# Exponent of an attention pass issued behind the FFN work that is woven into the same pass

## The reference, cut to what matters

```python
qkv    = einsum('nlck,cki->nlci', layernorm(x), Wqkv) + bqkv
scores = einsum('nlcd,nled->nldce', q, k) / 8      # 32x32 for each of 64 d
attn   = softmax(scores, axis=-1)
ctx    = einsum('nldcm,nlcd->nldm', attn, v)
x      = x + layernorm(ctx @ Wout + bout)          # per channel
gate, up = xn @ w_gate.T, xn @ w_up.T              # hidden 8192, xn = layernorm(x)
x      = x + layernorm((silu(gate) * up) @ w_down.T)
```

## Time and profile before

| | us |
|---|---|
| median of 3 runs | 7090.63 (7042.11 to 7113.12) |
| profiled execution, device time | 6908.24 |
| its span, slowest core (4) | 6906.7 (all cores 6886.3 to 6906.7) |
| mean granted TensorE clock of the cores | 0.797 to 0.801 |

### The profile page before, as it was taken

The page is one execution under the profiler, slowest core; times in us unless marked ns, Lnnn a source line. Parts: engine busy times, 40 slices in busy tenths (PEclk is TensorE's granted clock), DMA queues, the critical chain, the costliest instruction groups (busy, mean ns, idle before and its releaser), DMA issues.

```text
span 6906.7 us, 47532 instructions; the slowest of 8 cores (6886.3 to 6906.7 us)
## 1 busy us (share of the span) xinstructions
PE 3316.8 (48%) x15536; PEld 1510.1 (22%) x15536; DVE 3227.3 (47%) x3680; ACT 2051.3 (30%) x2953; POOL 16.4 (0%) x34
## 2 busy tenths in 40 slices
PE   0000011011076767650776767506858576069994
PEld 0000000000032323220333333203323232034441
DVE  0000026866756554637555546475655565631112
ACT  0000024344333434332333343324343433222110
POOL 0000000000000000000000000000000000000000
PEclk9999999555587888875787878757879787579997
DMA  9999940000042323221322322212313222134442
GB/s 112 110 109 109 109 56 6 1 6 6 0 122 73 101 83 104 79 64 34 107 89 79 104 87 96 62 36 92 104 61 122 70 101 68 36 113 143 153 141 88
DMA packets 177940, 558.92 MB, mean 81 GB/s; under 512 B 49568, under 2 KB 65952, under 8 KB 174496
## 3 DMA queue, kind: packets, MB, share of 16 engines
q1 hardware_dynamic: 171840, 444.69, 19.7%
q0 software_dynamic: 5856, 111.18, 14.4%
HBM read 641.83 MB, written 125.83 MB: 111 GB/s over the span
## 4 chain that ended last, share of the span: by engine, by line
DVE 31%; PE 23%; ACT 17%; another core or an unknown queue 14%; issue 9%; DMA 6%; DVEq 1%; ACTq 0%; SPq 0%
PE dps L415 10%; DVE es_sb L321 7%; DVE ctx_sb L330 6%; PE gps L353 5%; ACT es_sb L765 5%; PE ups L363 5%; DVE zs_sb L743 4%; DVE zs_sb L737 4%; DVE es_sb L728 3%; DMA wd_sb<-wdc 3%; ACT kd_sb L262 2%; ACT m_sb L379 2%; ACT e_sb L376 2%; DMA x2s_sb<-x2h 2%
## 5 line engine op out<-in xcount | busy, mean ns | idle before, releaser
L353 PE MATMUL gps<-xn_sb,wg_sb 128*128 128x512 bf16 x4096 | 1106.6, 432 | 347.8 <-DVE gated_sb L388 332.8
L415 PE MATMUL dps<-gated_sb,wd_sb 128*128 128x512 bf16 x4096 | 928.8, 385 | 100.7 <-DMA wd_sb<-wdc 49.2
L765 ACT ACTIVATE es_sb<-es_sb 128x4096 bf16<-128x4096 bf16 x256 | 921.9, 3601 | 23.1 <-DVE es_sb L728 23.1
L363 PE MATMUL ups<-xn_sb,wu_sb 128*128 128x512 bf16 x4096 | 925.8, 379 | 0.0
L249 PE MATMUL mps<-xn_sb,wqkv_sb 128*128 128x128 bf16 x512 | 72.3, 302 | 1511.2 <-DVE xn_sb L795 1460.0
L754 ACT ACTIVATE rz_sb<-zf_sb 128x128 bf16<-128x128 bf16 x256 | 79.0, 308 | 2343.3 <-DVE zf_sb L747 2343.3
L383 DVE TENSOR_TENSOR t_sb<-m_sb,gps 128x512 bf16<-128x512 bf16 x256 | 176.1, 688 | 1232.5 <-ACT m_sb L379 1232.5
L202 DVE TENSOR_SCALAR st_sb<-mps 1x128 f32<-1x128 f32 x48 | 13.4, 278 | 1441.4 <-PE mps L189 1441.4
L353 PEld LDWEIGHTS gps<-xn_sb,wg_sb 128*128 128x128 bf16 x4096 | 437.2, 108 | 987.7 <-issue 629.0
L321 DVE TENSOR_TENSOR es_sb<-es_sb,u_sb 128x4096 bf16<-128x4096 bf16 x256 | 586.8, 2292 | 28.4 <-DVE u_sb L312 2.3
L728 DVE TENSOR_TENSOR es_sb<-q_sb,kd_sb 128x4096 bf16<-128x4096 bf16 x256 | 586.0, 2290 | 24.4 <-DVE ctx_sb L330 0.9
(11 more groups left out here) (84 smaller groups left out, 2028.0 us busy)
## 6 DMA issues: line engine op xcount, KB each, us to landing
wg_sb<-wgc SPq DMA_DIRECT2D x256, 512.0 KB, 3.5
wu_sb<-wuc SPq DMA_DIRECT2D x256, 512.0 KB, 3.4
wd_sb<-wdc SPq DMA_DIRECT2D x256, 512.0 KB, 3.4
wgc<-wgH POOLq DMA_DIRECT2D x4, 8192.0 KB, 438.8
wuc<-wuH POOLq DMA_DIRECT2D x4, 8192.0 KB, 514.8
wdc<-wdH POOLq DMA_DIRECT2D x4, 8192.0 KB, 591.0
yT<-outs_sb SPq DMA_DIRECT2D x64, 256.0 KB, 2.9
xb_sb<-xH POOLq DMA_DIRECT2D x16, 512.0 KB, 8.6
```

The lines of the kernel that those rows point to most:

```text
L353: return tn.matmul(out=gps[pb].ap(), lhsT=wg_sb[pb].ap()[:, ft * 128:(ft + 1) * 128], rhs=xn2_sb.ap()[:, ft * W:(ft + 1) * W], start=(ft = ...
L363: return tn.matmul(out=ups[pb].ap(), lhsT=wu_sb[pb].ap()[:, ft * 128:(ft + 1) * 128], rhs=xn2_sb.ap()[:, ft * W:(ft + 1) * W], start=(ft = ...
L415: return tn.matmul(out=dps[pb].ap(), lhsT=wd_sb[wb].ap()[:, sh * 128:(sh + 1) * 128], rhs=gated_sb.ap()[:, ht * W:(ht + 1) * W], start=(ht ...
L765: ta = plan.op("A", lambda a, buf=buf: a.activation(out=buf.ap(), in_=buf.ap(), func=AF.Exp, scale=0.125), deps=[last[f"s_{c}_{j}"]], inc="A")
```

## The change

`emit_exp(j)` moves from ahead of `pull(2)` to behind `pull(2)` and `emit_uP(c, j - 1)`:

```diff
                 if j >= 1:
                     emit_z(j - 1)
                     emit_rz(j - 1)
-                if j < NJ:
-                    emit_exp(j)
                 pull(2)
                 if j >= 1:
                     emit_uP(c, j - 1)
+                if j < NJ:
+                    emit_exp(j)
```

## The result

| | us |
|---|---|
| changed kernel, median of 9 runs | 6597.89 (6585.88 to 6766.36) |
| kernel before, median of 10 runs | 6916.89 (6903.4 to 7113.12) |
| ratio of the two | 0.9551, 95% interval 0.9527 to 0.9574 |
| changed kernel, profiled execution, its span | 6596.17, 6594.6 |

By the ratio the change takes 4.5% off. The medians differ by 319 us, the profiled executions by 312; 315 had been forecast. In some executions of either kernel the cores of one die, sometimes of both, show a lower granted clock and the time is 1 to 3% longer; the three runs known of before, 7042 to 7113 us, were as long as such executions, and the ratio leaves these out.

The account below looks back on a forecast made before the run. In gu passes a loop of waits through ACT and DVE was the bound, not PE. 3 windows x (101.4 + 3.5) = 315 us, taken from the runs' median 7090.6, gave 6776 us, range 6670 to 6880.

Parts of the forecast that it names:

- The 182 us: Whole kernel: the runs' median lies 182 us above the profiled execution; carried over unchanged, may shrink or grow by some 100.
- the gain of a pass: Passes with two gu atoms: their first ACT instruction starts 3.50 us earlier, so a pass takes 17.08 us instead of 20.58.
- the cover: Gu passes: DVE's t1, gated, uP(j-1) and s(j+1) hide the moved exponent before z(j), with 5.3 us left over.
- the count: Gu passes of a window: 28 gain 3.5 us and 2 gain 1.7 us, 101.4 us a window.
- pass 0: First pass of a chunk with gu atoms: no gain, and no loss, with 0.7 us to spare before z(0).
- the second chunk from pass 1 to 9: Pass 1 moves the start of the down matmuls 3.5 us; first-half down passes, set by PE, and pass 9 gain zero.
- PE between two ends: Gu passes: PE idles 3.1 us at the high clock level, some 0.3 us at the low; the chain stays the bound.
- A: Rival: PE becomes the bound of the gu passes, 18.5 us a pass; gain 190 us, 6900 us; chance 0.06.
- B: Rival: granted clock falls to 0.80 in all dense stretches; 6940 us profiled, 7123 on the runs' scale; chance 0.05.
- C: Rival: z(j) waits for the moved exponent and the 3.5 us come back; 7091 us; chance 0.03.
- D: Rival: PE's clock stays at the low level in gu passes; +640 us, 7730 us; chance 0.02.
- ln4, bc4, down: Other passes: ln4 zero, the bc4 pass gains 3.5 us, first-half down passes cost zero, or 14 us in all if uncovered.

Follow-up runs that it names:

- e7: Kernel before, its order kept, with 6 further ACT instructions ahead of the exponent in gu passes from j = 1: 7288.1 us profiled, against 6912.7.
- e6: Changed order with 12 further ACT instructions ahead of the late exponent in gu passes from j = 1: 6905.0 us, ratio 0.9993 to the kernel before.
- e4: Against the kernel before, both atoms issued right after z(j-1), ahead of rz(j-1) and the exponent: 6317.2 us, ratio 0.9154.
- e2: Against the kernel before, the exponent issued late only in passes whose atoms contain a gu: 6605.0 us, ratio 0.9554.
- e3: Against the kernel before, the exponent issued late only in passes without a gu atom: 6924.8 us, ratio 0.9994.

## Why the prediction was right or wrong

**Wrong: the time itself.** 6776 us was forecast, 6670 to 6880 as its range; measured is 6598. The step that failed is the last of the sum: "I carry the difference over as it is". The 182 us between the profiled execution and the median of three runs were no property of the kernel. Of ten runs of before six lie at 6903 to 6919, by the profiled execution at 6908, and the other four, the three known runs among them, at 7042 and more. Had the sum ended on the profiled execution, 6593, it would have missed by 5 us. The hint was there: the profiled execution lay 134 us under the lowest of the runs, whose own spread is 71. The range let the 182 us shrink by some 100; they went altogether. With a difference like that unexplained, the range had to reach down to 6593; it stopped 77 us above. The mechanism and the gain were right.

**Right: the gain of a pass.** 3.50 us from the row of the exponent's place; passes went from 20.58 to 17.08 us. e7 shows the same from the other side.

**Right: the cover.** 5.3 us forecast, 5.4 in the timeline, 5.3 by e6.

**Right: the count.** 101.4 us a window were forecast for the gu passes; in the mean of the eight cores the three windows gave 103.6, 103.8 and 100.6. On the slowest cores alone it is 107.9 (48.8 + 23.8 + 35.3), 101.5 and 98.5, so the 6.5 us over in the first window are scatter of single cores. Of pass 0 no loss was forecast and none appears: from s(0) to s(1) it takes 16.7 us in chunk 4 (17.6 before), 17.3 in chunk 8 (16.9) and 17.5 in chunk 12 (17.6).

**Wrong in the parts, right in the sum: the second chunk from pass 1 to 9.** The forecast gave pass 1 its 3.5 us, the down passes and pass 9 zero. In fact pass 1 gained 3.5 us (17.3 to 13.8 in chunk 5), pass 2 lost 6.9 (12.4 to 19.3), and pass 9 gained 7.6 (29.1 to 21.5). The loss is z(1), which now waits for an exponent that stands behind the copy of the first down, and this copy waits for its matmuls:

```profile
2283.97 0.60 ACT L427 ACTIVATE y_sb<-dps 128x512 bf16<-128x512 f32 x1 [11.40 <-PE dps L415]
...
2284.47 3.61 ACT L765 ACTIVATE es_sb<-es_sb 128x4096 bf16<-128x4096 bf16 x1
2288.18 1.23 DVE L737 TENSOR_TENSOR zs_sb<-es_sb 128x2048 bf16<-128x2048 bf16 x1 [7.70 <-ACT es_sb L765]
```

Passes 1 to 9 together gained 3.6, 3.9 and 1.7 us in the three windows (mean of 8 cores), about the 3.5 forecast. That PE sets these passes, the reason given, held for their sum; it did not hold pass by pass.

**Right: PE between two ends.** The idle time of a pass was to be 3.1 us, or 0.3 if the low clock level came. It came: 3.11 us in one pass with the next group at 5.15 us, then 1.57 and a full-speed group, and so on in turn. The pass stays at 17.1 us in both, as the sum had it. The waits for `gated` are fewer, shorter and half in total (the earlier trace rows had 332.8, 78, 5.9):

```profile
PE gps L353 <- DVE gated_sb L388: 165.1, 72, 3.5
```

**The rivals.** A, PE as the bound, did not come with this change, but does in e4. B: the last window (6100 to 6500 us) ran at a granted clock of 0.99 (0.98 before), and in the gu and down chunks 4, 5 and 6 the clock rose from 0.79, 0.84 and 0.81 to 0.85, 0.87 and 0.86, on the slowest core of each execution. The current limit in the Trainium skill (TensorE: Matmul & The Clock Gate, Part 1) does not show in this trace: all eight cores ran that part of the last window at 0.96 to 0.99. C did not come: in the first and third chunks of the FFN windows (4, 6, 8, 10, 12, 14) no z waits for L765. It begins, by e6, where 5.3 us more stand ahead of the exponent, and has eaten the gain at 8.6 us. D: the low level never lasted past the first group: all 256 groups of L363 ran at the high one.

**ln4, bc4, down.** The 3.5 us of bc4 are there, in its pass, in all three windows (e2 and e3 above). Whole fourth chunks gained 3.3, 4.2 and 0.9 us in the mean of the eight cores; single cores vary by more than that (from -7.7 to 7.7 us in the last one). The new wait in the down passes costs nothing in the sum (e3).

## What to carry to other kernels

On an engine that takes its list in order, an instruction costs its full time in every loop that passes through the place where it stands, whether or not the loop needs its result: look for the instruction that ends long before it is read, and that another engine's work queues behind. Find its reader, measure how long the reader has other work, and put it behind the queue if that is more than its duration. Then repeat: the next one here, rz, was worth another 4%. And end the sum on the execution that its rows come from: if profile and runs differ by more than the effect of a stage and nothing explains it, the difference is a case of its own in the range.

## What the runs showed of the hardware

- TensorE's clock after an idle time, read from the groups of 16 matmuls of L353 in the changed kernel: after 3.10 or 3.11 us, 24 of 27 groups took 5.1 to 5.3 us, with 7 or 8 matmuls at the pace of the 1.2 GHz level; the other three, and all 29 after 1.3 to 1.8 us, took 3.61 us, the high level throughout. Two of three groups after 2.09 us were slow as well. In the kernel before, the shortest idle time with a low level behind it was 3.65 us. So a shorter idle time than the rows of before could show has its price.
- The idle time alone does not set that price: in the kernel before, the nine groups after 3.65 to 3.85 us took 6.3 to 6.5 us, 13 or 14 matmuls slow, the eleven after 4.85 to 5.27 us only 4.9 to 5.6 us, 6 to 10 slow, and those after 5.28 to 5.90 us had anything from 6 to 14 slow. What does set it, no run here shows.
- The exponent ran beside other DVE instructions than before (`u` times `es` and the sum) and both kept their durations, 3.60 us the exponent and 2.29 us each of the others: no contention between ACT and DVE on these operands.
